# A two-layer graph network on one core: the destination table in a stage of its own, and one Relu for a step's columns

## The reference, cut to what matters

```python
# layer 0
mean_edge = segment_sum(edge_attr, dst) / max(count, 1)
x1 = layernorm(x + softplus([x, mean_edge, glob] @ W.T) - log 2)
# layer 1
h = relu(ln(x1 @ W1 + b1, g1, bt1))
ef = concat(h[src], h[dst])                       # per edge
w = sigmoid(relu(ef @ We1 + be1) @ We2 + be2)     # one weight per edge
aggr = segment_sum(w * h[src], dst)
gate = sigmoid(concat(h, aggr) @ Wg + bg)
out = layernorm(x1 + ln(gate * aggr + (1 - gate) * h, g2, bt2))
```

## Time and profile before

| | us |
|---|---|
| three runs | 2412.96, 2417.81, 2413.09 (median 2413.09) |
| profiled execution, its own time | 2396.84 |
| its span | 2395.1 |
| busy DVE | 1792.9 (75%) |
| busy PE / PEld | 1667.4 (70%) / 1483.3 (62%) |
| busy POOL | 1450.4 (61%) |
| busy ACT | 1199.2 (50%) |

### The profile page before, as it was taken

One profiled execution on the slowest core, in us unless ns is written; L12 is line 12 of the kernel. 1 busy time (PEld: TensorE's weight loads), 2 busy tenths in 40 slices (PEclk: granted clock), 3 DMA queues, 4 the chain that ended last, 5 costly groups with the idle time before them and its releaser, 6 DMA issues.

```text
span 2395.1 us, 41524 instructions
## 1 busy us (share of the span) xinstructions
PE 1667.4 (70%) x13036; PEld 1483.3 (62%) x13037; DVE 1792.9 (75%) x4116; ACT 1199.2 (50%) x3254; POOL 1450.4 (61%) x1438
## 2 busy tenths in 40 slices
PE   4998885754553476777667777677777877777780
PEld 3777764644553466667666676666766766677660
DVE  7777774959875688887888877888777676777756
ACT  1555543747650355554555545555544444444325
POOL 4444400667776666666666666666666666666645
PEclk9999996886665567766777767767677676766765
DMA  7898983154444345545454555555555555555411
GB/s 269 294 302 298 317 295 117 43 182 133 124 122 138 107 144 158 153 146 157 145 154 145 155 152 167 156 165 152 164 158 165 158 165 157 170 157 165 137 39 54
DMA packets 279175, 394.05 MB, mean 165 GB/s; under 512 B 75169, under 2 KB 178724, under 8 KB 278827
## 3 DMA queue, kind: packets, MB, share of 16 engines
q1 hardware_dynamic: 217267, 226.52, 29.9%
q0 software_dynamic: 57408, 156.84, 22.4%
q10 hardware_dynamic: 4280, 8.03, 1.0%
HBM read 376.07 MB, written 15.12 MB: 163 GB/s over the span
## 4 chain that ended last, share of the span: by engine, by line
PE 29%; issue 16%; DVE 13%; DVEq 10%; another core or an unknown queue 6%; POOL 6%; ACT 2%; DMA 1%; ACTq 0%; SPq 0%; POOLq 0%
PE bank L551 7%; PE bank L1410 6%; PE bank L1433 5%; POOL x_rows L917 4%; PE bank L1412 4%; DVEq L539 3%; PE bank L527 3%; DVEq L1918 2%; PE bank L1441 2%; DVEq L1947 2%; DVE sums L1903 2%; DVE bank L537 2%; DVE bank L532 1%; PE bank L1388 1%
## 5 line engine op out<-in xcount | busy, mean ns | idle before, releaser
L917 POOL DMA_INDIRECT x_rows<-src_table,lane_src x900 | 896.3, 996 | 443.1 <-issue 244.7
L1410 PE MATMUL bank<-ring,sums 128*128 128x128 f32 x980 | 290.2, 370 | 137.9 <-issue 134.2
L1412 PE MATMUL bank<-ring,sums 128*128 128x128 bf16 x1470 | 238.9, 259 | 208.7 <-issue 207.7
L917 POOL DMA_INDIRECT ring<-src_table,lane_src x296 | 293.9, 993 | 144.4 <-issue 79.8
L555 DVE TENSOR_TENSOR sums<-sums,bank 128x128 f32 (+1 forms) x814 | 206.6, 254 | 173.2 <-issue 93.0
L1412 PEld LDWEIGHTS bank<-ring,sums 128*128 128x128 bf16 x1470 | 156.3, 119 | 267.7 <-issue 254.3
L1903 DVE TENSOR_SCALAR sums<-sums,ring 128x128 f32<-128x128 f32 x490 | 148.0, 367 | 228.2 <-remote 228.1
L537 DVE SCALAR_TENSOR_TENSOR bank<-bank,we_all 128x512 f32<-128x512 f32 x423 | 279.2, 692 | 14.8 <-remote 2.7
L1410 PEld LDWEIGHTS bank<-ring,sums 128*128 128x128 f32 x980 | 199.6, 242 | 145.3 <-issue 141.4
L551 PEld LDWEIGHTS bank<-weighted,x_rows 128*128 128x128 f32 x1800 | 279.5, 243 | 12.4 <-issue 12.3
L551 PE MATMUL bank<-weighted,x_rows 128*128 128x40 f32 x1800 | 276.3, 322 | 11.6 <-issue 11.6
(11 more groups left out here) (252 smaller groups left out, 3098.2 us busy)
## 6 DMA issues: line engine op xcount, KB each, us to landing
ring<-in_edge_attr SPq DMA_DIRECT2D x195, 512.0 KB, 5.1
ring<-rel_table SPq DMA_DIRECT2D x74, 512.0 KB
ring<-cell_table SPq DMA_DIRECT2D x121, 256.0 KB
ring<-src_table SPq DMA_DIRECT2D x144, 128.0 KB
x_rows<-src_table,lane_src POOLq DMA_INDIRECT x900
ring<-dst_table SPq DMA_DIRECT2D x299, 32.0 KB
ring<-src_table SPq DMA_DIRECT2D x104, 64.0 KB
src_table<-ring SPq DMA_DIRECT2D x12, 512.0 KB, 3.7
```

The lines of the kernel that those rows point to most:

```text
L917: eng.indirect_dma_start(gathered(c)[:, j, :], None, src_table, bass.IndirectOffsetOnAxis(ap=lane_src[:, t:t + 1], axis=0)).then_inc(gathe ...
L1410: eng.matmul(o, src_hot[:, u % 2, e], src_part[:, u % U_SLOTS, col_block(u, i), :], start=True, stop=False, skip_group_check=True)
L1412: last = eng.matmul(o, dst_hot[:, u % 2, e], base_dst[:, k % 2, s, :], start=False, stop=(s == PARTS - 1), skip_group_check=True)
```

## The change

The source table and the destination table are made one after the other. PE, ACT, DVE and SP each run all source work of the 13 groups and then the destination work. The destination tile moves from two slots in `ring` to four slots in the last 3072 columns of `counts`; the source tile gets a fourth slot (and with it the last stage, which shares it). Destination products alternate between PSUM banks 5 and 7. `sort_start` comes before the destination work on DVE, and `hot_t(0)` waits for all destination writes, because the sort's tiles overlie the four slots. The gathers no longer wait for `part2`. In `sort_columns` one Relu covers all columns of a step. Three pairs of dependent operations (POOL's gain and offset, the last stage's gain, ACT's softplus) are separated by a drain in place of a semaphore.

```diff
-    SRC_SLOTS, HOT_PAIRS = 3, 3
+    SRC_SLOTS, DST_SLOTS, HOT_PAIRS = 4, 4, 3
...
-        dst_at = at[0]
-        dst_out = temp(GC * PARTS // 2, BF16)
+        assert at[0] <= 21 * BANK
+        dst_at = at[0] - 2 * GC
+        dst_out = counts[:, columns - DST_SLOTS * GC * PARTS // 2:columns].bitcast(BF16).rearrange("p (s c) -> p s c", s=DST_SLOTS)
...
+        def dst_bank(g):
+            return bank[5 + 2 * (g % 2)]
...
 # SP
-            run_stages(n_groups, [(0, src_table_out), (DST_AT - NORM2_AT - 2, dst_table_out)])
+            for g in range(n_groups):
+                src_table_out(g)
+            for g in range(n_groups):
+                dst_table_out(g)
             eng.wait_ge(done("pad_rows"), 1)
             eng.dma_start(dst_table[padded * PARTS:dst_rows * PARTS, :], pad_rows[:, :]).then_inc(done("dst_table_pad"), 16)
             loaded(eng, "dst_table_pad")
-            for k in range(2):
-                loaded(eng, f"dst_table{k}", slot_uses(k, 2))
+            for k in range(DST_SLOTS):
+                loaded(eng, f"dst_table{k}", slot_uses(k, DST_SLOTS))
+            loaded(eng, f"src_table{SRC_SLOTS - 1}", slot_uses(SRC_SLOTS - 1, SRC_SLOTS))
...
 # POOL
-                eng.tensor_tensor(z, z, wide["g1"]...to_broadcast([P, nb, P]), ALU.mult).then_inc(done("gain"), 1)
-                need(eng, "gain", g)
+                eng.tensor_tensor(z, z, wide["g1"]...to_broadcast([P, nb, P]), ALU.mult)
+                eng.drain()
...
-                if c == own_slots:
-                    eng.wait_ge(done("part2"), n_groups)
...
 # ACT
-                eng.activation(t, pre[:, g % 2, 0:n], ACT.Abs).then_inc(done("act"), 1)
-                eng.wait_ge(done("act"), 2 * g + 1)
-                eng.activation(t, t, ACT.Exp, scale=-1.0).then_inc(done("act"), 1)
-                eng.wait_ge(done("act"), 2 * g + 2)
+                eng.activation(t, pre[:, g % 2, 0:n], ACT.Abs)
+                eng.drain()
+                eng.activation(t, t, ACT.Exp, scale=-1.0)
+                eng.drain()
...
-                if g >= 2:
-                    loaded(eng, f"dst_table{g % 2}", g // 2)
-                eng.activation(part(g, 0), bank[5]..., ACT.Copy).then_inc(done("part0"), 1)
+                if g >= DST_SLOTS:
+                    loaded(eng, f"dst_table{g % DST_SLOTS}", g // DST_SLOTS)
+                eng.activation(part(g, 0), dst_rows_of(g), ACT.Copy).then_inc(done("part0"), 1)
...
-                (NORM2_AT + 3, src_rows), (DST_AT + 1, part0), (DST_AT + 2, part1), (NORM2_AT + 1, relu),
+                (NORM2_AT + 3, src_rows), (NORM2_AT + 1, relu),
                 (5, lambda g: inverse_std(g, "moments2", rstd2, moments2, "rstd2", "norm2"))])
+            run_stages(n_groups, [(0, part0), (1, part1)])
...
-                for k, t in enumerate(ts):
-                    last = eng.activation(cols_[:, k, :], cols_[:, k, :], ACT.Relu, bias=ones[:, 0:1], scale=-1.0)
-                last.then_inc(done("col_hot"), 1)
+                all_ = cols_[:, 0:len(ts), :].rearrange("p k q -> p (k q)")
+                eng.activation(all_, all_, ACT.Relu, bias=ones[:, 0:1], scale=-1.0).then_inc(done("col_hot"), 1)
...
 # PE
             def dst_mm(g):
-                need(eng, "rest", g - 1)
-                per_block(g, bank[5], ..., we1_dst[:, :], added=1).then_inc(done("dst_mm"), 1)
+                need(eng, "rest", g - 2)
+                per_block(g, dst_bank(g), ..., we1_dst[:, :], added=1).then_inc(done("dst_mm"), 1)
             run_stages(n_groups, [
-                (4, x1_turn), (5, w1_mm), (0, mean_mm), (NORM2_AT + 2, src_mm), (NORM2_AT + 1, h_turn), (DST_AT, dst_mm)])
+                (4, x1_turn), (5, w1_mm), (0, mean_mm), (NORM2_AT + 2, src_mm), (NORM2_AT + 1, h_turn)])
+            for g in range(n_groups):
+                dst_mm(g)
...
 # DVE
-                (4, norm1), (1, pre_), (2, soft_sum), (3, moments1_), (NORM2_AT, norm2), (5, moments2_),
-                (DST_AT + 1, rest_), (DST_AT + 2, part2)])
+                (4, norm1), (1, pre_), (2, soft_sum), (3, moments1_), (NORM2_AT, norm2), (5, moments2_)])
...
                 if q == 0:
-                    sort_start()
+                    for k in range(DST_SLOTS):
+                        loaded(eng, f"dst_table{k}", slot_uses(k, DST_SLOTS))
...
+            sort_start()
+            run_stages(n_groups, [(0, rest_), (1, part2)])
             run_stages(n_steps, [(0, hot_t), (3, weigh_), (2, logits), (5, acc2)])
```

More of the change, by code:

```diff
@@ L314, in gnn_pair @@
         src_i = counts[:, phase_at + 2 * P + 2 * tokens:phase_at + 2 * P + 3 * tokens].bitcast(I32)
+        assert phase_at + 2 * P + 3 * tokens <= columns - DST_SLOTS * GC * PARTS // 2
         RIDE = COLS * P
@@ L589, in w1_bank, with dst_rows_of, dst_parts @@
             return bank[2 + 4 * (g % 2)]
+        def dst_bank(g):
+            return bank[5 + 2 * (g % 2)]
+        def dst_rows_of(g):
+            return dst_bank(g)[:, 0:blocks_of[g] * P].rearrange("p (b f) -> p b f", b=blocks_of[g])
+        def dst_parts(g):
+            return dst_out[:, g % DST_SLOTS, 0:blocks_of[g] * PARTS * P].rearrange("p (b s f) -> p b s f", s=PARTS, f=P)
         far_turned = bank[1][0:WP, 0:J * P // 2].bitcast(BF16).rearrange("w (j e) -> w j e", j=J)
@@ L886, in gain @@
                 z = z1[:, g % 2, 0:nb * P].rearrange("p (b f) -> p b f", b=nb)
-                eng.tensor_tensor(z, z, wide["g1"][:, :].unsqueeze(1).to_broadcast([P, nb, P]), ALU.mult).then_inc(done("gain"), 1)
-                need(eng, "gain", g)
+                eng.tensor_tensor(z, z, wide["g1"][:, :].unsqueeze(1).to_broadcast([P, nb, P]), ALU.mult)
+                eng.drain()
                 eng.tensor_tensor(z, z, wide["bt1"][:, :].unsqueeze(1).to_broadcast([P, nb, P]), ALU.add).then_inc(done("offset"), 1)
@@ L947, in _ @@
                 need(eng, "out_norm", g)
-                eng.tensor_tensor(z, z, wide["g2"][:, :].unsqueeze(1).to_broadcast([P, nb, P]), ALU.mult).then_inc(done("gain2"), 1)
-                need(eng, "gain2", g)
+                eng.tensor_tensor(z, z, wide["g2"][:, :].unsqueeze(1).to_broadcast([P, nb, P]), ALU.mult)
+                eng.drain()
                 need(eng, "out_rows", g - END_SLOTS)
@@ L1103, in part @@
             def part(g, k):
-                return dst_out[:, g % 2, 0:blocks_of[g] * PARTS * P].rearrange("p (b s f) -> p b s f", s=PARTS, f=P)[:, :, k, :]
+                return dst_parts(g)[:, :, k, :]
             def part0(g):
@@ L1108, in part0 @@
                 need(eng, "dst_mm", g)
-                if g >= 2:
-                    loaded(eng, f"dst_table{g % 2}", g // 2)
-                eng.activation(part(g, 0), bank[5][:, 0:nb * P].rearrange("p (b f) -> p b f", b=nb), ACT.Copy).then_inc(done("part0"), 1)
+                if g >= DST_SLOTS:
+                    loaded(eng, f"dst_table{g % DST_SLOTS}", g // DST_SLOTS)
+                eng.activation(part(g, 0), dst_rows_of(g), ACT.Copy).then_inc(done("part0"), 1)
             def part1(g):
@@ L1368, in dst_mm @@
             def dst_mm(g):
-                need(eng, "rest", g - 1)
-                per_block(g, bank[5], lambda b: h_block(g, b), we1_dst[:, :], added=1).then_inc(done("dst_mm"), 1)
+                need(eng, "rest", g - 2)
+                per_block(g, dst_bank(g), lambda b: h_block(g, b), we1_dst[:, :], added=1).then_inc(done("dst_mm"), 1)
             run_stages(n_groups, [
-                (4, x1_turn), (5, w1_mm), (0, mean_mm), (NORM2_AT + 2, src_mm), (NORM2_AT + 1, h_turn), (DST_AT, dst_mm)])
+                (4, x1_turn), (5, w1_mm), (0, mean_mm), (NORM2_AT + 2, src_mm), (NORM2_AT + 1, h_turn)])
+            for g in range(n_groups):
+                dst_mm(g)
             eng.wait_ge(done("rest"), n_groups)
@@ L1713, in far_item @@
                 with eng.If(start < first + 1):
-                    eng.memset(shift[:, :], 0.0).then_inc(done("far_new"), 1)
+                    eng.memset(shift[:, :], 0.0)
                 eng.drain()
@@ L1801, in rest_ @@
                 nb = blocks_of[g]
-                three = dst_out[:, g % 2, 0:nb * PARTS * P].rearrange("p (b s f) -> p b s f", s=PARTS, f=P)
+                three = dst_parts(g)
                 r = rest[:, g % 2, 0:nb * P].rearrange("p (b f) -> p b f", b=nb)
@@ L1805, in rest_ @@
                 need(eng, "part2", g - 2)
-                eng.tensor_tensor(r, bank[5][:, 0:nb * P].rearrange("p (b f) -> p b f", b=nb), three[:, :, 0, :], ALU.subtract).then_inc(done("rest"), 1)
+                eng.tensor_tensor(r, dst_rows_of(g), three[:, :, 0, :], ALU.subtract).then_inc(done("rest"), 1)
             def part2(g):
                 nb = blocks_of[g]
-                three = dst_out[:, g % 2, 0:nb * PARTS * P].rearrange("p (b s f) -> p b s f", s=PARTS, f=P)
+                three = dst_parts(g)
                 r = rest[:, g % 2, 0:nb * P].rearrange("p (b f) -> p b f", b=nb)
@@ L2014 @@
 NORM2_AT = 6
-DST_AT = 10
 DVE_BLOCKS = 2
```

2 lines of the change are left out of this document (1 added, 1 removed).

## The result

The changed kernel takes 2423.62 us (median of nine runs, 2419.43 to 2427.98) against 2414.18 for the kernel before (nine runs, 2412.62 to 2417.81): a ratio of 1.0036, 95% interval 1.0026 to 1.0046. It is slower by 9 us, where 2407.8 was forecast, and outside the range (2396 to 2418). The profiled execution took 2424.69 (span 2423.0).

A forecast was written before the change was run, and what follows sets the result against it. No engine bounds the span alone; PE, issue time, DVE and POOL share it. First logits 5.3 us earlier, the Relu and other parts nothing: 5.3 off the median 2413.09 gives 2407.8 us, range 2396 to 2418.

The forecast's parts named there:

- The table stage: Source work without the destination's: group 12's norm2 at 497.8, 8.2 us earlier; last source write issued at 502.7.
- the sort's gate: On DVE, sort_start ahead of rest(0) waits for POOL's iotas, done at 505.7; rest(0) begins at 508.9.
- the start of the gathers: POOL's first gather, once the last source write has landed: near 506.2, 23 us earlier.
- the transfers of the destination stage: Destination writes beside gathers: 1.9 us a group, four slots cover the 5 us to landing; last part2 at 532.3.
- the gathers' removed wait: POOL's gathers no longer waiting for part2: slot 6's gather came 27 us after it, so nothing, within 1 us.
- The slower rival: Destination stage becomes the bound: at 2.7 us a group, logits at 556.4, loss 4.3, time 2417.4; chance 0.15.
- The clock itself: PE in the destination stage: begins slow and ends fast, 1.6 us a group with three at 2.7.
- the way from there to the first window loads: SP after the last part2: 5.8 us before, taken as 5.0 after the change, window loads at 537.3.
- The base of the sum: Gain of 5.3 us taken off the median 2413.09, not only the profiled 2396.84: 2407.8 instead of 2391.5.
- 5.3 us go through whole: Edge loop: first logits come 5.3 us earlier, everything after keeps its old pace, so the full gain stays.
- It doesn't reach the end: Rival: PE's issue waits in the loop, 16% of the chain, could swallow a few us: 2413; chance 0.1.
- The Relu: ACT in sort_columns: one Relu at 2.2 us for ten costing 3.6; saving 1.4 a step only lengthens ACT's wait.

The follow-up runs named there:

- eight gathers first: Changed kernel with POOL waiting for the last part2 after eight gathers: 2395.43 us, 0.9940; on a chip without remote waits 2189.52 us, 1.0002.
- the break in the kernel before: Kernel before, POOL waiting for the first step's logits after 16 of its first 32 gathers: 2193.02, 2192.72 and 2193.58 us (1.0024, 1.0026, 1.0018).
- 64 rows a gather: Changed kernel whose first 32 gathers fetch 64 rows each instead of 128: 2188.86, 2190.98 and 2189.32 us (1.0003, 1.0008, 0.9996).

## Why the prediction was wrong

**The table stage, the sort's gate, the start of the gathers: right.** Last norm2 497.2 (497.8), last source write issued at 504.70 (502.7), iotas to 506.8 (505.7), rest(0) 509.9 (508.9), gathers 508.9 (506.2).

**The failed step: the transfers of the destination stage.** "A slot comes free after four groups (7.6 us), against 5 us from a write's issue to landing under load" and with it "I take 1.9: DMA's price". I priced the gathers beside the stage by their bytes alone. Writes issued by 517.77 and 519.18 let part0 go on at 530.96 and 550.57, 13 and 31 us later, not 5. Their bytes were gone from the queue by 526, and half the bytes in the gathers changed next to nothing: what the price left out is the time until a landing is known. Without a long train the step was right: with eight gathers first the last part2 ends at 532.9, 1.8 us a group from 509.24, and the first logits stand at 548.62, against 532.3, 1.9 and 546.8. The term for the gathers' removed wait ("Nothing, within 1 us either way") fell too, though by what it did not look at: it asked for the slot's data only, and not for what a longer train does to others. Restoring that wait gives back 9 of the 28 us that separate the changed kernel from the version with eight gathers first; the 24 gathers that still start inside the stage bring the rest.

**The slower rival named the right place and not the mechanism.** It had the stage become the bound, at 2.7 us a group through PE's clock, and 2417.4. The stage did become the bound, at 4.1 us a group ((563.6 - 509.9) / 13). PE's products were done long before: ACT's waits for PE in it stay under 3 us. The clock itself went as the prediction took it: eight passes took 2.08 us at 511.18 and 513.72 and 1.16 us from 516.04 on, until ACT's first long wait left PE without work.

**Two small readings.** The last part2 of the earlier trace rows ends at 536.24 + 0.89 = 537.1, not 536.7, so the way from there to the first window loads was 5.4 us and not 5.8. And 384 KB are 0.393 MB: at 208 and 245 GB/s a write takes 1.89 and 1.60 us, not 1.85 and 1.57. Neither moves the forecast beyond half a microsecond.

**The base of the sum.** Taking the gain off the median, 16 us above the profiled execution, looked like caution and hid a question. Of 47 runs of the kernel before on two chips 10 lie between 2396.1 and 2406.3, the others between 2410.5 and 2419.8. The kernel before with one Relu, profiled in an execution of 2409.2, shows what a usual one has and the earlier trace rows has not. PE, then ACT and DVE, just after the train's last gather (571.60):

```profile
569.94 0.27 PE L527 MATMUL bank<-ring,onehot_t 120*128 120x128 bf16 x1 [1.11 <-issue]
571.35 0.28 PE L527 MATMUL bank<-ring,onehot_t 120*128 120x128 bf16 x1 [1.15 <-issue]
572.76 0.27 PE L527 MATMUL bank<-ring,onehot_t 120*128 120x128 bf16 x1 [1.14 <-issue]
```

```profile
575.58 3.61 ACT L1141 ACTIVATE sums<-sums,pos 128x196 bf16<-128x196 bf16 x10 [16.72 <-remote]
575.58 1.49 DVE L1859 TENSOR_TENSOR sums<-sums 128x1280 bf16<-128x1280 bf16 x1 [16.46 <-remote]
```

Its second logits come at 584.22 where the profiled kernel before has 565.28. PE, which by the profile waits for nothing there, issues its matmuls one by one with 1.1 us between them, so it isn't only the news of a landing that is late. If this is the same effect, the kernel before usually meets it at the start of the loop, and the changed one meets it in the stage instead: 28 us are lost there against the undisturbed start, and some 16 no longer lost later. That leaves 12, where 9 were measured; the difference is within the spread of either kernel's runs. That the 16 us are this effect in every usual run is not shown: it is inferred from this one profile, and the test, the break in the kernel before, ran three times on chips without the effect.

**The gain where nothing stalls.** Without remote waits the changed kernel is not faster either (1.0014). In its own trace the first reduce of logits is at 557.40, no earlier than in the kernel before with a break on the same chip (556.86; the break waits for just these logits). Other versions of the changed kernel do have the head start and still gain nothing. On the first of these chips the reduce stands at 551.84 (eight gathers first) and 550.58 (64 rows a gather) against 555.29, with ratios of 0.9999 and 1.0003; on the last at 552.56 against 556.60, with 0.9996. So a head start of 3.5 to 4.7 us at the first logits is gone by the end. The forecast's "5.3 us go through whole" fails on these chips, and the rival "It doesn't reach the end" is what happened there, though not shown by the cause that it named; what binds the loop's first steps wasn't resolved.

**The Relu: right.** One over 1960 columns took 1.93 us (2.2 taken) in place of 3.60, and is worth nothing: 0.9992 alone, 2424.51 without it against 2423.62 with it, and without it in the version with eight gathers first 0.9999, where that version has 1.0002. The same step's ACT in the kernel before, then with eight gathers first:

```profile
596.85 0.30 ACT L1132 ACTIVATE weight<-logit,be_all 128x8 f32<-128x8 f32 x1 [3.11 <-DVE logit L541]
...
600.71 3.60 ACT L1144 ACTIVATE sums<-sums,ones 128x196 bf16<-128x196 bf16 x10
```

```profile
593.36 0.30 ACT L1152 ACTIVATE weight<-logit,be_all 128x8 f32<-128x8 f32 x1 [4.76 <-DVE logit L544]
...
597.23 1.93 ACT L1164 ACTIVATE sums<-sums,ones 128x1960 bf16<-128x1960 bf16 x1
```

ACT's wait for the same logits grew from 3.11 us to 4.76, by the 1.65 saved.

## What to carry to other kernels

Starting a train of indirect gathers earlier is not always free even where its data has room: ask which waits on other queues fall inside it, and try sending only as many as the next consumer needs before those waits are over. Compare when a transfer's bytes moved with when its waiter went on: that tells a late landing from late news of it. Where a profiled execution and the median are 0.7% apart, look for what differs between executions before a gain is taken off either. A reading that rests on "remote" or "issue" waits has to be checked on more than one chip.

## What the runs showed of the hardware

- On some chips a train of gathers at one every 1.25 us (0.95 of work and 0.30 between) is accompanied by late releases on other engines: 8.7 and 18.5 us in the stage, and 16.7 us at the loop's start, there behind a train whose last 14 gathers were as close. The last such wait ends 0.6 to 3.7 us after the train's last gather (five traces), the first one in the stage ends inside the train. Halving the gathers' bytes changes next to nothing. The queue that carried the awaited writes had been empty since 526 (but for a later write) when ACT went on at 550.57. Unbroken trains of 32, 40 and 64 gathers at one every 1.42 to 1.44 us had no such wait. What is shared is not known.
- The kernel before takes 2412 to 2414 us (median) in the three sessions of runs that came first and 2189 to 2190 us in the three that came later, on other chips. The version with eight gathers first has logits every 11.8 us from 1010 to 1153 on the one kind and, with column Relus, every 8.9 to 10.8 us on the other, with no remote wait at all: the remote waits of the loop, not only those of the stage, are gone. Whether it is the chip or something that changed with time can't be told.
- The TensorE clock's granted mean over an execution was 0.71 to 0.74 in the slower sessions and 0.75 to 0.77 in the others; it was 0.50, the 1.2 GHz level, while PE had nothing to do (541 to 551 above).
